# Second stage of a graph kernel: no merging between the two chunks of a step, every add behind the landing of the one ahead of it and behind two gathers

## The chip, the cores and the metric

One core of a Trainium2 chip runs the whole kernel in one launch. The metric is device time in microseconds (us), the median over runs. Engines: TensorE (PE; PEld is its weight load), VectorE (DVE), ScalarE (ACT), GpSimd (POOL), SyncE (SP, which here only issues DMAs).

## The reference

Four graph layers over the same 3125 nodes, 32 features and 100,000 edges (sorted by `dst`), each a residual `x = x + layer(relu(layernorm(x)))`:

```
_L0: agg = segment_sum(edge_attr, row, 3125); BN(relu([x, agg] @ W1.T + b1)) @ W2.T + b2
_L1: R = relu(dist * w1 + b1) @ w2 + b2                 # per edge, radial weights
     msg = R (x) Y(rel_vec) (x) features[src]           # per edge, 32 values
     out = zeros.at[dst].add(msg)
_L2: three rounds of  out = clip(0.9 * segment_sum(norm * out[row], col) + 0.1 * y, 0, 1)
_L3: three rounds of  z = BN(relu(segment_sum(wn * z[src], dst)))   # edges with a self loop per node
```

Layers L2 and L3 are done as products with dense adjacency matrices (sum of weights and number of edges for each pair src, dst), which the kernel builds itself during L0 and L1.

## The kernel before

The edges stand in 784 chunks of 128 (`CH`), of which 782 hold edges (`USED`). The program has three stages.

**First stage (L0).** Steps of four chunks; not touched by the change.

**Second stage (L1).** 196 steps (`STEPS`) of four chunks, in pairs of buffers `q = s % 2`. In step `s` of `phase1`:

- POOL fetches 128 rows of node features for each of the four chunks by an indirect DMA (`gather`, L593).
- DVE forms cross and dot products from them (L1433 is its first instruction of a step), multiplies by the radial weights (L1448, L1452), sums (L1462), and forms the values to be scattered (`products`, L1290).
- ACT builds one-hot matrices of `dst` (L668, L673); PE makes the radial weights of the step ahead (`radial`, L988) and sums the messages by node (`scatter`, L923).

**The adjacency** is a table `both` of (weight, count) pairs in DRAM, 8 bytes for each pair of nodes. Each of the 782 chunks is added to it by one indirect DMA that accumulates in place (`add(c)`, L585): 128 rows of 8 bytes. An edge that has the same key (src, dst) as another of the same chunk would be lost or doubled, so equal keys are merged first: `compare` on ACT (L656, L660) makes 128x128 matrices `same` of equal keys, DVE masks them (`mark_earlier`, L1268), PE sums the weights of equal edges (`merge`, L858, L862), and DVE writes values and rows to scatter to (`entries`, `entry_places`, L1276 to L1283). In the second stage this is done for two chunks in one go, with four matrices (chunk i against chunk j), so that the two chunks of a pair share no row, and their two adds may be under way together. The first 392 adds belong to the first stage and merge four chunks in another way.

**Order on POOL.** The stage's DMAs stand in one stream, written out without a loop: after two steps' gathers, each round issues the four gathers of step s+1 and then the two adds of the pair of step s-2 (`BEHIND`). The first add of a pair waits for both adds of the pair before to have landed, the second waits for the second add of that pair only. A step's first gather waits for `s_terms` (DVE has used the buffer two steps back).

**Third stage.** SP waits for all adds and for the last sums of the second stage, and then loads `both` back (L505), from which the dense layers L2 and L3 go on.

## Time and profile before

| | |
|---|---|
| median of 3 runs | 3463.08 us (3460.28 to 3467.24) |
| the profiled execution's own time | 3467.37 us |
| its span in the trace | 3465.3 us |
| PE, DVE, ACT, POOL busy, share of the span | 86%, 79%, 66%, 62% |
| second stage, first to last of its DVE work | about 1064 to 2820.6 us |

Busy time is given by engine. An engine that waits for a semaphore, or that stands between two instructions, is idle in it. For an indirect DMA the row of POOL is the time in which POOL makes the transfer's descriptors; the data land later.

### The profile page before, as it was taken

The numbers are of one execution on the slowest core, as the hardware profiler recorded it, in microseconds if no ns is written. First come the engines' busy times: TensorE is split into PE (matmuls) and PEld (weight loads), VectorE is DVE, ScalarE is ACT, GpSimd is POOL, SyncE is SP. The second block draws the span as 40 slices with busy tenths as digits, with TensorE's granted clock in tenths as the row PEclk, the third lists the DMA queues.
The fourth block names the chain that finished last, engine by engine and source line by source line (L and its number), as shares of the span: only waits on it lengthen the run. The fifth ranks groups of instructions, "written<-read, shape, count | busy, mean of one in ns | idle before, by whom it ended". The sixth has DMA issues, their size and how long they took to land. (4 is left out here: it accounts for less than half of the span.)

```text
span 3465.3 us, 69301 instructions
## 1 busy us (share of the span) xinstructions
PE 2974.6 (86%) x19703; PEld 2370.4 (68%) x19703; DVE 2742.9 (79%) x6018; ACT 2280.7 (66%) x3192; POOL 2141.3 (62%) x1629
## 2 busy tenths in 40 slices
PE   3888788988856999999999999999999976657657
PEld 3677677777745888888888888888888851113257
DVE  6678988888856999999999999999999973441065
ACT  3678688888836888888888888888888842220000
POOL 4048888888877777777777777777777730000000
PEclk9899899999977999999999999999999997798778
DMA  9943222222222333333333333333333359998940
GB/s 400 419 154 38 12 15 15 15 16 16 15 25 41 53 53 52 50 53 51 50 53 51 50 53 51 51 53 52 50 53 52 50 187 426 426 391 342 373 172 6
DMA packets 265695, 388.67 MB, mean 112 GB/s; under 512 B 149903, under 2 KB 200838, under 8 KB 259254
## 3 DMA queue, kind: packets, MB, share of 16 engines
q0 software_dynamic: 149184, 120.78, 20.7%
q1 hardware_dynamic: 100034, 195.42, 16.6%
q10 hardware_dynamic: 16416, 71.74, 5.1%
q8 instruction: 28, 0.46, 0.1%
q14 instruction: 33, 0.27, 0.0%
HBM read 260.01 MB, written 127.78 MB: 112 GB/s over the span
## 5 line engine op out<-in xcount | busy, mean ns | idle before, releaser
L585 POOL DMA_INDIRECT both<-kept x782 | 1333.0, 1705 | 439.8 <-issue 194.6
L923 PEld LDWEIGHTS ps<-prod,big 128*128 128x128 f32 x7840 | 1133.9, 190 | 137.7 <-DVE prod L1290 133.0
L923 PE MATMUL ps<-prod,big 128*128 128x170 f32 x7840 | 1183.2, 310 | 22.5 <-DVE prod L1290 17.4
L593 POOL DMA_INDIRECT kept<-feat_dram,kept x782 | 760.8, 973 | 243.2 <-issue 233.1
L668 ACT ACTIVATE big<-iota_b,kept 128x640 f32<-128x640 f32 x1029 | 779.0, 815 | 13.6
L914 PE MATMUL ps<-prod,onehot 128*128 128x320 f32 x3920 | 684.5, 325 | 81.2 <-DVE prod L1320 79.6
L914 PEld LDWEIGHTS ps<-prod,onehot 128*128 128x128 f32 x3920 | 597.7, 194 | 112.9 <-DVE prod L1320 84.5
L673 ACT ACTIVATE big<-big 128x2560 f32<-128x2560 f32 x196 | 458.0, 2337 | 277.2 <-PE ps L923 277.1
L988 PE MATMUL ps<-w2mix,kept 65*128 65x384 f32 x1568 | 559.3, 500 | 21.7 <-ACT kept L720 20.4
L1462 DVE TENSOR_REDUCE kept<-kept 128x80 f32<-128x1280 f32 x392 | 561.4, 1471 | 0.0
L988 PEld LDWEIGHTS ps<-w2mix,kept 65*128 65x128 f32 x1568 | 284.2, 191 | 179.7 <-issue 25.5
L1452 DVE TENSOR_TENSOR kept<-ps,kept 128x384 f32<-128x384 f32 x784 | 395.3, 544 | 0.0
L616 POOL DMA_INDIRECT prod<-both,row_idx x8 | 7.8, 977 | 526.2 <-DVE row_idx L1570 512.4
L1320 DVE TENSOR_TENSOR prod<-kept 128x1280 fp32r<-128x1280 f32 x196 | 291.9, 1489 | 4.3
L1311 DVE TENSOR_SCALAR onehot<-iota_b,kept 128x640 fp32r<-128x640 f32 x539 | 291.4, 593 | 0.0
L673 ACT ACTIVATE onehot<-big 128x640 fp32r<-128x640 f32 x196 | 171.1, 873 | 182.4 <-PE ps L914 173.7
L1129 PE MATMUL ps<-big,zring 128*32 128x512 f32 (+3 forms) x400 | 183.5, 615 | 118.6 <-DMA big<-both 106.8
L1448 DVE TENSOR_TENSOR kept<-ps,kept 128x512 f32<-128x512 f32 x392 | 266.1, 679 | 0.0
L643 ACT ACTIVATE kept<-ps,kept 128x128 f32<-128x128 f32 (+2 forms) x588 | 223.3, 477 | 0.0
L1129 PEld LDWEIGHTS ps<-big,zring 128*32 128x32 f32 x400 | 45.3, 124 | 256.8 <-issue 242.3
L1520 DVE TENSOR_REDUCE row_max<-big 128x1 f32<-128x1600 f32 x50 | 91.0, 1819 | 160.0 <-DMA adj_c<-kept 107.6
L765 ACT ACTIVATE kept<-big 128x1600 f32<-128x1600 f32 x50 | 82.2, 1648 | 187.0 <-issue 83.2
(235 smaller groups left out, 3028.9 us busy)
## 6 DMA issues: line engine op xcount, KB each, us to landing
both<-big POOLq DMA_DIRECT2D x40, 1910.0 KB, 91.2
big<-both SPq DMA_DIRECT2D x24, 1600.0 KB, 11.8
big<-both SPq DMA_DIRECT2D x24, 1528.0 KB, 13.2
kept<-keys_dram SPq DMA_DIRECT2D x196, 128.0 KB, 3.0
kept<-in_wT SPq DMA_DIRECT2D x196, 128.0 KB
adj_c<-kept ACTq DMA_DIRECT2D x42, 400.0 KB, 31.6
kept<-adj_c SPq DMA_DIRECT2D x9, 1600.0 KB, 22.4
adj_w<-kept ACTq DMA_DIRECT2D x16, 800.0 KB, 33.6
```

The costliest lines, as they stand in the source:

```text
L585: pool.indirect_dma_start(both, bass.IndirectOffsetOnAxis(ap=sc_idx[:, c:c + 1], axis=0), sc_val[:, c // 2, c % 2, :], None, compute_op=AL ...
L593: pool.indirect_dma_start(gath[:, s % 2, k, :], None, feat_dram, bass.IndirectOffsetOnAxis(ap=src_i[:, 4 * s + k:4 * s + k + 1], axis=0)). ...
L668: act.activation(dist[:, k, :], iota_b[:, :], ACT.Square, scale=-1.0, bias=bcol[:, ds(4 * s + k, 1)]).then_inc(s_dist[n], 4 // len(ks))
L673: act.activation(to[:, q, 0:len(ks), :], dist[:, 0:len(ks), :], ACT.Relu, scale=-1.0, bias=1.0).then_inc(s_oh[n], 1)
L914: mm = pe.matmul(ps[:, SUM0[part], 0:HI * 2 * FEAT], onehot0[:, q, k, part * P:(part + 1) * P], prod0[:, q, k, :, :].rearrange("p a m -> p ...
L923: mm = pe.matmul(part_sums(part, MSG), onehot[:, q, k, part * P:(part + 1) * P], prod[:, q, k, 0:HI * MSG], start=False, stop=False, skip_ ...
L988: mm = pe.matmul(ps[:, 4 + k, 0:384], hidT[:, q, k * P:(k + 1) * P], w2mix[:, :], start=True, stop=True)
L1311: ins = V.tensor_scalar(onehot0[:, q, k, :], iota_b[:, :], b_src[:, ds(4 * s + k, 1)], None, ALU.is_equal)
L1320: V.tensor_tensor(prod0[:, q, :, :, :], high0[:, ds(4 * s, 4), :].unsqueeze(3) .broadcast_to([P, 4, HI, 2 * FEAT]), rows0[:, 4 * k4:4 * k4 ...
L1448: V.tensor_tensor(T[:, :, 0:256].rearrange("p k (o x) -> p k o x", o=16), ps[:, 4 + 2 * g:6 + 2 * g, 0:256].rearrange("p k (o x) -> p k o ...
L1452: ins = V.tensor_tensor(T[:, k, 256:640].rearrange("p (u i x) -> p u i x", u=8, i=3), ps[:, 4 + 2 * g + k, 256:384].rearrange("p (u x) -> ...
L1462: V.tensor_reduce(res[:, q, 2 * g:2 * g + 2, 0:40], terms[:, g, :, :].rearrange("p k (o x) -> p k o x", x=16), AX, ALU.add).then_inc(s_red, 1)
```

## The change

`compare` makes two matrices instead of four (each chunk only against itself: two squares of 128 columns instead of two of 256, one relu of 256 instead of 512), and `merge` has two matmuls fewer (four instead of six). `mark_earlier` reads two adjacent matrices instead of the first and the fourth. Since two chunks of a pair may now hold the same row, each add of the second stage waits for the landing of the one just ahead of it (`s_add` of the other parity), and on POOL one add now stands behind each two gathers instead of two adds behind four. The number of gathers and adds is the same.

```diff
             def add(c):
 
                 pool.wait_ge(s_idx, c // 2 + 1)
-                if c >= CH // 2 and c % 2 == 0:
-                    pool.wait_ge(s_add[1], 16 * (c // 2))
-                if c >= 2:
+                if c >= CH // 2:
+                    pool.wait_ge(s_add[(c - 1) % 2], 16 * ((c + 1) // 2))
+                if 2 <= c <= CH // 2:
                     pool.wait_ge(s_add[c % 2], 16 * (c // 2))
...
             for s in range(STEPS + BEHIND):
-                if s + 1 < STEPS:
-                    gather(s + 1, range(min(4, USED - 4 * (s + 1))))
-                if s >= BEHIND:
-                    for c in range(2 * (STEPS + s - BEHIND), min(2 * (STEPS + s - BEHIND) + 2, USED)):
+                for k in range(4):
+                    if s + 1 < STEPS and 4 * (s + 1) + k < USED:
+                        gather(s + 1, k)
+                    c = 2 * (STEPS + s - BEHIND) + k // 2
+                    if s >= BEHIND and k % 2 and c < USED:
                         add(c)
...
                 for i in range(2):
-                    act.activation(key_gap[:, 2 * i * P:(2 * i + 2) * P], keyrow[:, q, 0:2 * P], ACT.Square, scale=-1.0,
+                    act.activation(key_gap[:, i * P:(i + 1) * P], keyrow[:, q, i * P:(i + 1) * P], ACT.Square, scale=-1.0,
                                    bias=key[:, ds(2 * d + i, 1)]).then_inc(s_gap, 1)
...
-                act.activation(same[:, q, 0:4, :].rearrange("p b e -> p (b e)"), key_gap[:, 0:4 * P], ACT.Relu,
+                act.activation(same[:, q, 0:2, :].rearrange("p b e -> p (b e)"), key_gap[:, 0:2 * P], ACT.Relu,
                                scale=-1.0, bias=1.0).then_inc(s_same, 1)
...
                 for j in range(2):
-                    pe.matmul(o[:, j, 0:1], same_tri[:, q, j, :], ones_bf[:, :], start=(j == 0), stop=False,
+                    pe.matmul(o[:, j, 0:1], same_tri[:, q, j, :], ones_bf[:, :], start=(j == 0), stop=True,
                               skip_group_check=True)
-                    for i in range(2):
-                        lo = 0 if (i, j) == (0, 1) else 1
-                        mm = pe.matmul(o[:, j, lo:7], same[:, q, 2 * i + j, :],
-                                       wparts[:, ds(2 * d + i, 1), lo:7].rearrange("p c v -> p (c v)"),
-                                       start=False, stop=(i == 1), skip_group_check=True)
+                    mm = pe.matmul(o[:, j, 1:7], same[:, q, j, :],
+                                   wparts[:, ds(2 * d + j, 1), 1:7].rearrange("p c v -> p (c v)"),
+                                   start=False, stop=True, skip_group_check=True)
```

POOL's stream at the second stage's first rounds with adds, before: L593 is a gather, L585 an add, and the semaphores `entries_added0` and `entries_added1` count the landings of adds with even and odd numbers.

```order
418 L593 DMA kept<-feat_dram,kept 128x96 [waits terms_ready]
419 L593 DMA kept<-feat_dram,kept 128x96 x3
420 L585 DMA both<-kept 9779712x2 [waits entries_added0,entries_added1,scatter_rows_ready]
421 L585 DMA both<-kept 9779712x2 [waits entries_added1,scatter_rows_ready]
422 L593 DMA kept<-feat_dram,kept 128x96 [waits terms_ready]
423 L593 DMA kept<-feat_dram,kept 128x96 x3
```

The same place of the change, where a gather is L592 (the file is one line shorter from there on). One add now follows each two gathers, and it waits for the add of the other parity.

```order
418 L592 DMA kept<-feat_dram,kept 128x96 [waits terms_ready]
419 L592 DMA kept<-feat_dram,kept 128x96
420 L585 DMA both<-kept 9779712x2 [waits entries_added0,entries_added1,scatter_rows_ready]
421 L592 DMA kept<-feat_dram,kept 128x96 x2
422 L585 DMA both<-kept 9779712x2 [waits entries_added0,scatter_rows_ready]
423 L592 DMA kept<-feat_dram,kept 128x96 [waits terms_ready]
424 L592 DMA kept<-feat_dram,kept 128x96
425 L585 DMA both<-kept 9779712x2 [waits entries_added1,scatter_rows_ready]
```

The end of POOL's second stage, before: behind the last two gathers stand the last six adds, in pairs.

```order
1186 L593 DMA kept<-feat_dram,kept 128x96 [waits terms_ready]
1187 L593 DMA kept<-feat_dram,kept 128x96
1188 L585 DMA both<-kept 9779712x2 [waits entries_added0,entries_added1,scatter_rows_ready]
1189 L585 DMA both<-kept 9779712x2 [waits entries_added1,scatter_rows_ready]
1190 L585 DMA both<-kept 9779712x2 [waits entries_added0,entries_added1,scatter_rows_ready]
1191 L585 DMA both<-kept 9779712x2 [waits entries_added1,scatter_rows_ready]
1192 L585 DMA both<-kept 9779712x2 [waits entries_added0,entries_added1,scatter_rows_ready]
1193 L585 DMA both<-kept 9779712x2 [waits entries_added1,scatter_rows_ready]
```

The end of the change: the same six adds, each of which waits for the one just ahead.

```order
1378 L592 DMA kept<-feat_dram,kept 128x96 [waits terms_ready]
1379 L592 DMA kept<-feat_dram,kept 128x96
1380 L585 DMA both<-kept 9779712x2 [waits entries_added1,scatter_rows_ready]
1381 L585 DMA both<-kept 9779712x2 [waits entries_added0,scatter_rows_ready]
1382 L585 DMA both<-kept 9779712x2 [waits entries_added1,scatter_rows_ready]
1383 L585 DMA both<-kept 9779712x2 [waits entries_added0,scatter_rows_ready]
1384 L585 DMA both<-kept 9779712x2 [waits entries_added1,scatter_rows_ready]
1385 L585 DMA both<-kept 9779712x2 [waits entries_added0,scatter_rows_ready]
```

## Rows read from the trace of the kernel before

**Rows 1.** The page, part 1: busy us, share of the span, instructions.
```profile
PE 2974.6 (86%) x19703; PEld 2370.4 (68%) x19703; DVE 2742.9 (79%) x6018; ACT 2280.7 (66%) x3192; POOL 2141.3 (62%) x1629
```

**Rows 2.** Busy us by stretch, with granted clock, DMA share and GB/s.
```profile
1600.00:2800.00 1200.00, 1184.85 (x7235) 990.52 (x7234) 1137.14 (x2680) 996.80 (x1341) 955.06 (x804) 1.00 0.32 51
```

**Rows 3.** Waits from 1600 to 2800 us: total us, times, longest us.
```profile
POOL kept L593 <- issue: 161.2, 529, 0.3
...
DVE kept L1433 <- DMA kept<-feat_dram,kept: 25.5, 93, 0.4
```

**Rows 4.** Groups by line, 1600 to 2800 us: busy us, mean ns, idle before.
```profile
L593 POOL DMA_INDIRECT kept<-feat_dram,kept x536 | 519.7, 970 | 163.3 <-issue 161.2 <-DMA both<-kept 2.1
L585 POOL DMA_INDIRECT both<-kept x268 | 435.8, 1626 | 81.7 <-issue 43.6 <-DVE kept L1283 38.1
```

**Rows 5.** POOL in order of time, one step: start us, us, instruction, [idle before].
```profile
2021.00 1.01 POOL L593 DMA_INDIRECT kept<-feat_dram,kept  x1 [0.30 <-issue]
2022.31 0.98 POOL L593 DMA_INDIRECT kept<-feat_dram,kept  x1 [0.30 <-issue]
2023.60 0.94 POOL L593 DMA_INDIRECT kept<-feat_dram,kept  x1 [0.30 <-issue]
2024.84 0.94 POOL L593 DMA_INDIRECT kept<-feat_dram,kept  x1 [0.30 <-issue]
2026.09 1.61 POOL L585 DMA_INDIRECT both<-kept  x1 [0.30 <-DVE kept L1283]
2028.00 1.58 POOL L585 DMA_INDIRECT both<-kept  x1 [0.30 <-issue]
```

**Rows 6.** All engines in order of time, DVE's start of the next step.
```profile
2027.52 0.26 DVE L1433 TENSOR_TENSOR kept<-kept 128x96 f32<-128x96 f32 x1 [0.33 <-DMA kept<-feat_dram,kept]
```

**Rows 7.** POOL where a long run of adds changes to gathers.
```profile
1055.73 1.54 POOL L585 DMA_INDIRECT both<-kept  x1 [0.30 <-issue]
1057.58 1.02 POOL L593 DMA_INDIRECT kept<-feat_dram,kept  x1 [0.30 <-issue]
...
1060.19 0.94 POOL L593 DMA_INDIRECT kept<-feat_dram,kept  x1 [0.30 <-issue]
```

**Rows 8.** POOL, the last gather of the stage that DVE held up.
```profile
1095.52 1.01 POOL L593 DMA_INDIRECT kept<-feat_dram,kept  x1 [0.49 <-DVE kept L1452]
```

**Rows 9.** POOL in the stage before, an add that waits for the second add ahead.
```profile
1041.08 1.54 POOL L585 DMA_INDIRECT both<-kept  x1 [0.34 <-issue]
...
1045.78 1.54 POOL L585 DMA_INDIRECT both<-kept  x1 [1.11 <-DMA both<-kept]
```

**Rows 10.** All engines at the second stage's end, in order of time.
```profile
2802.68 1.61 POOL L585 DMA_INDIRECT both<-kept  x1 [0.30 <-issue]
...
2803.30 0.17 PE L858 MATMUL ps<-ones_bf,kept 128*128 128x1 bf16 x1
...
2803.45 2.83 PE L988 MATMUL ps<-w2mix,kept 65*128 65x384 f32 x8
...
2804.59 1.63 POOL L585 DMA_INDIRECT both<-kept  x1 [0.30 <-issue]
...
2808.48 1.56 POOL L585 DMA_INDIRECT both<-kept  x1 [2.26 <-DMA both<-kept]
...
2810.34 1.54 POOL L585 DMA_INDIRECT both<-kept  x1 [0.30 <-issue]
...
2814.07 1.80 POOL L585 DMA_INDIRECT both<-kept  x1 [2.19 <-DMA both<-kept]
...
2816.17 1.54 POOL L585 DMA_INDIRECT both<-kept  x1 [0.30 <-issue]
2820.64 0.32 DVE L1484 TENSOR_TENSOR x<-x,ps 128x160 f32<-128x160 f32 x1 [6.19 <-PE ps L923]
2820.82 35.73 SPq L505 DMA_DIRECT2D big<-both  x10
```

**Rows 11.** The line of the adds, 1600 to 2800 us: durations in ns, min/median/max.
```profile
L585 POOL DMA_INDIRECT both<-kept x268: 1582/1610/1689, 1604.7 to 2798.2; - x134
```

More of the change, by code:

```diff
@@ L586, in add, with gather @@
                                         sc_val[:, c // 2, c % 2, :], None, compute_op=ALU.add).then_inc(s_add[c % 2], 16)
-            def gather(s, ks):
-                if s >= 2:
+            def gather(s, k):
+                if s >= 2 and k == 0:
                     pool.wait_ge(s_terms, 2 * (s - 1))
-                for k in ks:
-                    pool.indirect_dma_start(gath[:, s % 2, k, :], None, feat_dram,
-                                            bass.IndirectOffsetOnAxis(ap=src_i[:, 4 * s + k:4 * s + k + 1], axis=0)
-                                            ).then_inc(s_gath[s % 2], 16)
+                pool.indirect_dma_start(gath[:, s % 2, k, :], None, feat_dram,
+                                        bass.IndirectOffsetOnAxis(ap=src_i[:, 4 * s + k:4 * s + k + 1], axis=0)
+                                        ).then_inc(s_gath[s % 2], 16)
             pool.wait_ge(s_zeroed, 16 * (ZERO_PIECES + 1))
@@ L601, in _ @@
             pool.wait_ge(s_feat, 16)
-            gather(0, range(4))
+            for k in range(4):
+                gather(0, k)
             for s in range(STEPS + BEHIND):
-                if s + 1 < STEPS:
-                    gather(s + 1, range(min(4, USED - 4 * (s + 1))))
-                if s >= BEHIND:
-                    for c in range(2 * (STEPS + s - BEHIND), min(2 * (STEPS + s - BEHIND) + 2, USED)):
+                for k in range(4):
+                    if s + 1 < STEPS and 4 * (s + 1) + k < USED:
+                        gather(s + 1, k)
+                    c = 2 * (STEPS + s - BEHIND) + k // 2
+                    if s >= BEHIND and k % 2 and c < USED:
                         add(c)
@@ L1267, in mark_earlier @@
                 dve.wait_ge(s_ded, d - 1)
-                V.tensor_tensor(same_tri[:, q, 0:2, :], same[:, q, 0:4:3, :], earlier[:, :].unsqueeze(1).broadcast_to([P, 2, P]),
+                V.tensor_tensor(same_tri[:, q, 0:2, :], same[:, q, 0:2, :], earlier[:, :].unsqueeze(1).broadcast_to([P, 2, P]),
                                 ALU.mult).then_inc(s_tri, 1)
```

## The prediction

> **What bounds the kernel now.** Read the page first, part 1: PE is the busiest engine by far and POOL the least busy [rows 1]. That is an average over three stages, and the change touches the second alone. The chain that ended last is no help here, since on this page it can be followed only from 3128 us on, behind the stage. So take a stretch in the middle of the stage, 1600 to 2800 us. Of its 1200 us PE is busy 1184.85, DVE 1137.14, ACT 996.80 and POOL 955.06, at a granted clock of 1.00, the higher level of 2.4 GHz [rows 2]. By busy time PE would be the bound, and POOL would have 20% to spare.
>
> The waits say otherwise. Ahead of the gathers POOL's idle time comes in pieces of at most 0.3 us [rows 3], and ahead of the adds it is 81.7 / 268 = 0.30 on average [rows 4]. The groups give the sum too: gathers 519.7 busy and 163.3 idle before them, adds 435.8 and 81.7, together 1200.5 us of the 1200 [rows 4]. So POOL never waits for anybody; 0.30 us is what lies between two of its indirect DMAs in any case. The stretch holds 268 / 2 = 134 steps, so a step takes 1200.5 / 134 = 8.96 us, and that is POOL's own sum: four gathers, two adds, six gaps. DVE, on the contrary, waits at the head of its step for the gathered rows, in 93 of the 134 steps [rows 3]: the last gather starts at 2024.84 and DVE, after 0.33 us of waiting for it, at 2027.52 [rows 5, 6]. PE and ACT wait for DVE and for each other behind it. **POOL is the bound of the stage**, from the last gather that DVE held up, at 1095.52 [rows 8], to the stage's end. It covers 190 steps.
>
> Now look at one step of POOL closely [rows 5]. The four gathers do the same work, but take 1.01, 0.98, 0.94 and 0.94 us. The first after an add is 0.07 us longer, the second 0.04, and from the third on there is nothing more. The same stands where a run of nearly 400 adds ends: 1.02 for the first gather, 0.94 for the third [rows 7]. The adds have it too: 1.61 for the first after a gather, 1.58 for the second, 1.54 in a long run [rows 5, 7]. A change of kind costs POOL about 0.11 us over two instructions.
>
> **The change part by part.**
>
> *ACT.* Two squares and a relu with half the columns. ACT is busy 996.80 of 1200 us, so it has room already: 0 us. What hides it is POOL's step; nothing is late next.
>
> *PE.* Two bf16 matmuls fewer for each step. Six of them stand between 2803.30 and 2803.45, where the next matmul begins [rows 10], so two are worth 0.05 us a step. PE works in POOL's shadow: 0 us. Were PE the bound it would be 0.05 x 190 = 9.5 us less.
>
> *DVE.* As many instructions of the same size: 0 us.
>
> *The new wait for landing.* Behind it stand on POOL two gathers and the next add, and DVE's next step waits for these gathers. The trace before shows what a landing takes where POOL has nothing else to do: an add that starts at 2804.59 lets the next but one start at 2808.48, 3.89 us later; another at 2810.34 lets it start at 2814.07, 3.73 us later [rows 10]. In the changed stream the next add can't start earlier anyway than 1.61 + 0.30 + 1.01 + 0.30 + 0.98 + 0.30 = 4.50 us after the one ahead. So the wait is over 0.6 us before it could hold anything: 0 us a step. The bounds are 3.73 and, from the stage before, 4.70 us (1041.08 to 1045.78 [rows 9]), where two adds of a quick row of adds were under way together. At 4.70 each add would stall 0.20 us. I take 3.8, because the changed adds stand apart by two gathers and never share the queue with another add.
>
> By the Trainium skill ("DMA: Bandwidth & Descriptors", the section on the anatomy of a DMA on the GpSimd path), a small transfer of this kind has about 2.0 us of fixed cost, most of it the receipt of the write; as an estimate by that page the wait would end 2 us ahead of need, and the sum would be the same. The rows say 3.7 to 3.9, and only 0.6 us of cover is left.
>
> *The order on POOL.* Here is the cost. Six instructions a step as before, but four changes of kind instead of two. The third and fourth gather, 0.94 and 0.94, come to stand as first and second after an add, 1.01 and 0.98: + 0.07 + 0.04 = 0.11 us a step. Both adds now stand as first after a gather; the row of before has 1.61 and 1.58, which would be 0.03 more, but the group's mean of 1.626 [rows 4] lies above both, so the second is no cheaper on average: 0. Together 0.11 x 190 = 20.9 us. The bounds: 0 below, if the durations do not follow the position, and 0.14 x 190 = 26.6 above, with the adds' 0.03.
>
> *The end of the stage.* Six adds stand behind the last gather. Before, they ran in pairs, and from the first of them (2802.68) to SP's first load of the third stage (2820.82) it was 18.14 us; DVE saw PE's last sum at 2820.64, so both sides ended together [rows 10]. Now they go one by one: five times 3.73 to 3.89, and then from the last start to SP's load as before 4.65 us (2816.17 to 2820.82), or some 3.1 if that landing was a late one. That is 18.65 + 3.1 = 21.8 to 19.45 + 4.65 = 24.1 us, against 18.14: + 3.6 to 6.0, taken as 4.5. On the other side, an add now stands between the last gather of the last full step and the last two gathers, so this gather is 1.9 us nearer to the end, and DVE's and PE's last two steps with it: + 1.9, hidden beside the adds' 4.5. SP's loads wait for both, and the third stage waits for the loads.
>
> *Sum.* 20.9 + 4.5 = 25.4 us. Against the profiled execution's own 3467.37 us that is 3492.8. Its time is 4.3 above the median of the runs, so the forecast is 3463.1 + 25.4 = 3488.5, given as **3488 us**, 0.7% slower.
>
> **The rivals.**
>
> *A. One add does not undo what two gathers have set up.* In the trace an add between gathers always comes in twos or more, so what a single one does is not shown. If the cost of 0.07 is made of 0.03 for the instruction just ahead and 0.04 for the one before that, the first gather after a single add pays 0.03 and the second 0.04: 0.14 a step instead of 0.11. With the adds' 0.03 or without it that is 0.03 to 0.06 x 190 = 6 to 11 us, and with the end 10 to 16: 3473 to 3479 us. That the second instruction still pays speaks for it; that two gathers are already enough to make the next add dear (1.61 at 2802.68) speaks for neither.
>
> *B. The position costs nothing new.* The durations follow something else that the new order does not change, and only the end of the stage is left: 3463.1 + 4.5 = 3467.6, and 3465 if a part of it is hidden in the third stage. This is within 0.2%, which is 6.9 us and about what a measurement of this kernel can tell from no change. Against it speaks that two different places show the same 0.07 and 0.04.
>
> *C. The landing is not covered.* It decides from 4.50 us on. At the 4.70 of rows 9, each add stalls 0.20: 0.40 x 190 = 76 us more, 3564. A stall in one of four adds gives 19 us more, 3507. For it: the loads of SP lie in the same part of a step. Against it: 3.73 and 3.89, and an add in the new order has the same neighbours ahead (two gathers) as the first add of a pair before.
>
> *D. POOL is not the bound; its rows only fill the step.* Then PE is, at 1184.85 of 1200 us, and the two matmuls are a gain: 3463.1 - 9.5 = 3453.6, 0.3% faster, if PE's last step also hides the adds' end. Against it: POOL's gaps are 0.30 to the last digit and its gathers agree to 0.01 us in each position, which a stretched engine would not show, and DVE waits for the gathers. It would decide only if PE's own step were above 8.96 us.
>
> *E. The adds' durations move with what DVE does beside them.* They spread from 1.58 to 1.69 us [rows 11]. If the moved add fell wholly on 1.54 [rows 7] or on 1.68 instead of its mean of 1.626, it would be -0.09 or +0.05 a step, -16 or +10 us: 3472 to 3498. The Trainium skill ("SBUF — State Buffer", the section on its two separate sides) has a rule of that form: DVE and GpSimd take one port pair in turn for a whole instruction, DVE's with two operands in SBUF included. By this rule, the trace agrees as far as that the adds spread; the gathers, which stand beside DVE as well, do not.
>
> **How the numbers follow.** Forecast 3488, own range 3480 to 3496: 0.47. A: 0.20. B: 0.13. C: 0.07. D: 0.05. E: 0.08. The range 3466 to 3498 holds the forecast, A, E and the upper half of B; what it leaves out is C, D and the rest of B, some 0.18. Faster by over 0.2% are D and a sliver of B and E together: 0.06. Within 0.2% is B and the lower edge of A: 0.16. Slower: 0.78.
>
> **What the profile of the changed kernel would show.** POOL's rows in the middle of the stage: gather, gather, add, with 1.01, 0.98, 1.61 and gaps of 0.30; busy plus idle still the whole stretch; a step of 9.07 us. A shows as a first gather of 0.97, B as 0.94. C shows as gaps above 0.30 before adds, ended by the DMA both<-kept. D shows as POOL waiting for DVE, with a step below 8.96. DVE's idle time before its first instruction of a step should grow by what POOL's step does. The last six adds should start 3.7 to 3.9 us apart, and SP's load 22 to 24 us behind the first of them. The third stage should keep its length of 645 us. The prediction is wrong if the step is not 0.1 us longer, or if the gap before the adds is.

## The result, and the profile after

The changed kernel takes **3516.44 us** (median of 4 runs, 3510.75 to 3520.16), the kernel before on the same chip 3465.16 us. The ratio is 1.0149 (95% interval 1.0127 to 1.017): 51 us or 1.5% slower, twice the 25.4 us forecast, and above the range. The profiled execution took 3514.57 us, with a span of 3512.5, 47.2 more than that of before.

The page, part 1, answers to [rows 1], and busy time by stretch for 1600 to 2800 us to [rows 2]:

```profile
PE 2977.3 (85%) x19310; PEld 2377.0 (68%) x19311; DVE 2740.9 (78%) x6018; ACT 2198.1 (63%) x3192; POOL 2151.1 (61%) x1629
```

```profile
1600.00:2800.00 1200.00, 1156.39 (x6783) 972.30 (x6783) 1108.18 (x2612) 916.82 (x1307) 940.63 (x784) 0.99 0.31 50
```

Every engine does less in the same 1200 us. The stage has become slower without a busier engine, so something is waited for: ahead of an instruction, or inside one. The groups of POOL for the same stretch, against [rows 4] (busy us, mean ns of one, idle before them and what ended it):

```profile
L592 POOL DMA_INDIRECT kept<-feat_dram,kept x522 | 508.7, 974 | 159.2 <-issue 110.7 <-DMA both<-kept 48.5
L585 POOL DMA_INDIRECT both<-kept x262 | 433.5, 1655 | 100.5 <-issue 60.1 <-DVE kept L1282 22.3 <-DMA both<-kept 18.2
```

The stretch holds 262 / 2 = 131 steps; POOL's four sums make 1201.9 us, or 9.175 a step against 8.959. By terms: gathers 508.7 / 131 = 3.883 (before 3.878), adds 3.309 (3.252), idle time 259.7 / 131 = 1.982 (1.828). So + 0.005, + 0.057 and + 0.154, together 0.216 a step, and times 190 that is 41 us. (Busy and idle time fill any stretch, so the sum alone doesn't show that POOL is the bound. `z2_nudged_more`, below, does: there an add that takes 0.6 us longer makes the step 9.48 us.) The waits and the durations of the adds' line say how it is spread:

```profile
POOL both L585 <- issue: 60.1, 169, 1.5
...
DVE kept L1432 <- DMA kept<-feat_dram,kept: 53.9, 100, 2.1
...
POOL both L585 <- DMA both<-kept: 18.2, 20, 1.2
```

```profile
L585 POOL DMA_INDIRECT both<-kept x262: 1597/1607/2301, 1598.6 to 2798.0; - x131
```

Before, no idle time on POOL was above 0.3 us; now the longest ahead of an add is 1.5. And while the median add still takes 1607 ns, the longest takes 2301 instead of 1689 [rows 11]. Below, an add is called *stalled* when POOL stands idle for more than 0.35 us ahead of it (0.30 lie between two of its DMAs in any case), and *held* when it takes over 1.7 us. Two steps in order of time show both; these are the rows of POOL, SP and DVE's `products` from all engines' (start, duration, [idle before]):

```profile
1999.32 1.61 POOL L585 DMA_INDIRECT both<-kept  x1 [0.31 <-DVE kept L1282]
1999.40 0.87 DVE L1289 TENSOR_TENSOR prod<-high,kept 128x680 f32<-128x680 f32 x1 [0.23 <-DVE kept L1470]
...
2000.63 0.34 SPq L424 DMA_DIRECT2D kept<-keys_dram  x1
...
2001.23 0.98 POOL L592 DMA_INDIRECT kept<-feat_dram,kept  x1 [0.30 <-issue]
2001.86 0.49 SPq L468 DMA_DIRECT2D kept<-in_wT  x1
2002.51 0.95 POOL L592 DMA_INDIRECT kept<-feat_dram,kept  x1 [0.30 <-issue]
2004.44 1.60 POOL L585 DMA_INDIRECT both<-kept  x1 [0.98 <-DMA both<-kept]
2006.35 0.98 POOL L592 DMA_INDIRECT kept<-feat_dram,kept  x1 [0.31 <-issue]
2007.63 0.95 POOL L592 DMA_INDIRECT kept<-feat_dram,kept  x1 [0.30 <-DMA both<-kept]
...
2008.61 0.87 DVE L1289 TENSOR_TENSOR prod<-high,kept 128x680 f32<-128x680 f32 x1 [0.23 <-DVE kept L1470]
...
2008.89 2.07 POOL L585 DMA_INDIRECT both<-kept  x1 [0.30 <-issue]
...
2018.10 0.87 DVE L1289 TENSOR_TENSOR prod<-high,kept 128x680 f32<-128x680 f32 x1 [0.23 <-DVE kept L1470]
2018.25 2.19 POOL L585 DMA_INDIRECT both<-kept  x1 [0.30 <-issue]
```

*A landing that comes late.* The add at 1999.32 lets the next one start at 2004.44, 5.12 us later, with 0.98 instead of 0.30 us ahead of it. SP issued two loads of 128 KB, keys (L424) and weights (L468), 1.31 and 2.54 us after the add's start.

*An add that is held.* The add at 1999.32 starts 0.08 us before `products` and takes 1.61. Those at 2008.89 and 2018.25 start 0.28 and 0.15 us after it and take 2.07 and 2.19. Both end at the same distance from the start of `products`: 0.28 + 2.07 = 2.35 and 0.15 + 2.19 = 2.34 us.

Where nothing disturbs, the add is the first of the two by more (the same view, later):

```profile
2056.18 1.65 POOL L585 DMA_INDIRECT both<-kept  x1 [0.30 <-DVE kept L1282]
2056.57 0.87 DVE L1289 TENSOR_TENSOR prod<-high,kept 128x680 f32<-128x680 f32 x1 [0.23 <-DVE kept L1470]
```

The end of the stage answers to [rows 10]:

```profile
2841.10 1.60 POOL L585 DMA_INDIRECT both<-kept  x1 [0.30 <-issue]
2844.84 1.57 POOL L585 DMA_INDIRECT both<-kept  x1 [2.15 <-DVE kept L1282]
2850.03 1.54 POOL L585 DMA_INDIRECT both<-kept  x1 [3.61 <-DMA both<-kept]
2854.76 1.54 POOL L585 DMA_INDIRECT both<-kept  x1 [3.19 <-issue]
2858.47 1.54 POOL L585 DMA_INDIRECT both<-kept  x1 [2.17 <-DMA both<-kept]
...
2862.28 1.54 POOL L585 DMA_INDIRECT both<-kept  x1 [2.27 <-DMA both<-kept]
2867.16 20.07 SPq L505 DMA_DIRECT2D big<-both  x7
```

From the first of the six adds to SP's load it is 26.06 us, against 18.14: + 7.9 instead of the 4.5 forecast. Three of the five distances are 3.7 to 3.8 us, the other two 5.19 and 4.73. The third stage keeps its length, 3512.5 - 2867.2 = 645.3 us. With the 41 us above that makes 49 us, against 47.2 measured. In three other kernels with the same end it was less: 24.1 us in `x0_after_again`, 24.3 in `x2_late_loads` and 24.4 in `x5_late_split`, which is + 6.0 to 6.2.

### The profile page after: what moved, and what is told of

It reads as the page before. It is cut to its first block and busy times, and to the rows that moved or that the text cites. A ratio compares the mean times of both kernels' runs of the same rounds, so it can differ in the third digit from the quotient of the medians.

```text
span 3512.5 us, 68324 instructions
## 1 busy us (share of the span) xinstructions
PE 2977.3 (85%) x19310; PEld 2377.0 (68%) x19311; DVE 2740.9 (78%) x6018; ACT 2198.1 (63%) x3192; POOL 2151.1 (61%) x1629
## 5 line engine op out<-in xcount | busy, mean ns | idle before, releaser
L585 POOL DMA_INDIRECT both<-kept x782 | 1341.4, 1715 | 475.7 <-issue 224.8
L922 PEld LDWEIGHTS ps<-prod,big 128*128 128x128 f32 x7840 | 1152.6, 193 | 173.9 <-DVE prod L1289 166.8
L922 PE MATMUL ps<-prod,big 128*128 128x170 f32 x7840 | 1198.6, 313 | 64.8 <-DVE prod L1289 61.2
L592 POOL DMA_INDIRECT kept<-feat_dram,kept x782 | 762.3, 975 | 243.6 <-issue 164.9
```

The source lines that it names most:

```text
L585: pool.indirect_dma_start(both, bass.IndirectOffsetOnAxis(ap=sc_idx[:, c:c + 1], axis=0), sc_val[:, c // 2, c % 2, :], None, compute_op=AL ...
L592: pool.indirect_dma_start(gath[:, s % 2, k, :], None, feat_dram, bass.IndirectOffsetOnAxis(ap=src_i[:, 4 * s + k:4 * s + k + 1], axis=0)). ...
L922: mm = pe.matmul(part_sums(part, MSG), onehot[:, q, k, part * P:(part + 1) * P], prod[:, q, k, 0:HI * MSG], start=False, stop=False, skip_ ...
```

## The experiments

Ratios are against the kernel before on the same chip, with 95% intervals. In the expectations an odd add is the one behind a round's last gather, an even add the one in its middle.

**First: which part of the change costs?** Four kernels. `e1_order` has the merging and the waits of before and only the new order:

```diff
...
-                if s + 1 < STEPS:
-                    gather(s + 1, range(min(4, USED - 4 * (s + 1))))
-                if s >= BEHIND:
-                    for c in range(2 * (STEPS + s - BEHIND), min(2 * (STEPS + s - BEHIND) + 2, USED)):
+                for k in range(4):
+                    if s + 1 < STEPS and 4 * (s + 1) + k < USED:
+                        gather(s + 1, k)
+                    c = 2 * (STEPS + s - BEHIND) + k // 2
+                    if s >= BEHIND and k % 2 and c < USED:
                         add(c)
```

> Merging, matmuls and waits as in the kernel before; only POOL's order is the changed one (one add behind each two gathers). My first prediction (a change of kind costs 0.07 + 0.04 us) expects a step of 9.07 us and 3486 us. The theory that the wait for landing is the cost, and the order alone is free (changed kernel: gathers 0.98 and 0.95, adds 1.60 and 1.61), expects 0.98 x 2 + 0.95 x 2 + 1.60 + 1.61 + 6 x 0.305 = 8.90 us a step, no gap above 0.31 before an add, the end of the stage as before, and 3453 to 3462 us.

Measured: 3481.49 us, 1.0061 (1.004 to 1.0081). `e2_order_wait` has the new order and the new waits, with the merging of before (shown: the waits):

```diff
...
-                if c >= CH // 2 and c % 2 == 0:
-                    pool.wait_ge(s_add[1], 16 * (c // 2))
-                if c >= 2:
+                if c >= CH // 2:
+                    pool.wait_ge(s_add[(c - 1) % 2], 16 * ((c + 1) // 2))
+                if 2 <= c <= CH // 2:
                     pool.wait_ge(s_add[c % 2], 16 * (c // 2))
...
```

> The kernel before with the changed order and with the wait of each add for the one ahead, but with the merging of both chunks kept (four matrices, six matmuls). If order and wait are the whole cost, the time is that of the changed kernel, 3516, within 5 us. If the shorter compare on ACT matters, because it lets SP issue its 128 KB load of keys 0.2 us earlier and so into the landing of the add, this kernel has fewer stalls: gap before even adds 0.31 to 0.36 instead of 0.47, and 3475 to 3490 us.

Measured: 3496.32 us, 1.0097 (1.0073 to 1.0122). `e3_wide_compare` is the changed kernel with ACT's comparison as wide as before (the relu is widened too, and the readers of `same` take the first and the fourth matrix):

```diff
-                    act.activation(key_gap[:, i * P:(i + 1) * P], keyrow[:, q, i * P:(i + 1) * P], ACT.Square, scale=-1.0,
+                    act.activation(key_gap[:, 2 * i * P:(2 * i + 2) * P], keyrow[:, q, 0:2 * P], ACT.Square, scale=-1.0,
...
```

> The changed kernel, with ACT's compare as wide as before (four matrices made, two of them unused) and the matmuls of the change. It tells ACT's part from PE's. If the earlier load of keys is the cause, the time is that of the run with merging kept (3475 to 3490). If ACT has no part, it is 3516 within 5 us.

Measured: 3492.0 us, 1.0104 (1.0061 to 1.0147). `e4_pairs_wait` is the changed kernel with the order of before, where nothing covers the second add's wait:

```diff
...
-                for k in range(4):
-                    if s + 1 < STEPS and 4 * (s + 1) + k < USED:
-                        gather(s + 1, k)
-                    c = 2 * (STEPS + s - BEHIND) + k // 2
-                    if s >= BEHIND and k % 2 and c < USED:
+                if s + 1 < STEPS:
+                    gather(s + 1, range(min(4, USED - 4 * (s + 1))))
+                if s >= BEHIND:
+                    for c in range(2 * (STEPS + s - BEHIND), min(2 * (STEPS + s - BEHIND) + 2, USED)):
                         add(c)
```

> The changed kernel with the old order: four gathers, then two adds, each add waiting for the one ahead. The second add has no gather in front of it, so the landing stands open: 3.7 to 3.9 us from one start to the next instead of 1.92, which is 1.8 to 2.0 us a step and 340 to 380 us in all, 3810 to 3860 us. If a landing were covered by something else, it would stay near 3516.

Measured: 3894.32 us, 1.1254 (1.122 to 1.1289), above the 3810 to 3860 expected. Its POOL in order of time, one pair of adds:

```profile
2003.82 1.63 POOL L585 DMA_INDIRECT both<-kept  x1 [0.30 <-issue]
...
2007.73 1.59 POOL L585 DMA_INDIRECT both<-kept  x1 [2.29 <-DMA both<-kept]
```

3.91 us from add to add, in the middle of the stage; half of the pairs lie between 3.83 and 4.23 us, and the longest is 5.5. What follows from the four: the new order alone already costs. With the waits too it is a little more (the two intervals overlap), and the changed kernel, with the *shorter* work of ACT and PE, is slower still (its interval overlaps that of `e3_wide_compare`, and not those of `e1_order` and `e2_order_wait`; its second measurement, `x0_after_again` below, overlaps none of the three). No sum of fixed prices per instruction gives this: in `e1_order` a gather takes 974 ns on average as in the changed kernel, where I forecast dearer ones. In the profiled execution, the slowest of the seven, it is the adds that are longer, 3.374 us a step against 3.252, more than twice what the idle time has grown by (1.880 against 1.828):

```profile
L585 POOL DMA_INDIRECT both<-kept x263 | 443.7, 1687 | 87.1 <-issue 63.9 <-DVE kept L1284 23.2
```

`e1_order` isn't the order alone, though. In it the even add still waits for the odd one ahead, and there are now two gathers between them instead of four: that old wait has lost half of its cover, which is the time that passes between an add and the one that waits for it anyway.

**Second: loads and products.** My theory from here on: (1) SP's loads delay an add's landing beyond its cover; (2) an add that starts within `products` is held. Four edits of the changed kernel, and the kernel itself again. `x1_shifted` moves each add one gather ahead, away from `products`; `x2_late_loads` lets SP load a step's keys only when DVE has taken the step ahead; `x3_shifted_late` does both; `x4_split_products` forms the products by two instructions of half the size (edits in this order):

```diff
-                    if s >= BEHIND and k % 2 and c < USED:
+                    if s >= BEHIND and k % 2 == 0 and c < USED:
```

```diff
+                if not first(s):
+                    sp.wait_ge(s_vec, s - 1)
                 load_keys(s + STEPS, q)
```

```diff
-                V.tensor_tensor(prod[:, q, :, 0:HI * MSG].rearrange("p k (a m) -> p k a m", a=HI),
+                for k in (0, 2):
+                    V.tensor_tensor(prod[:, q, k:k + 2, 0:HI * MSG].rearrange("p k (a m) -> p k a m", a=HI),
...
```

> The changed kernel itself again, beside the others on one chip: 1.0127 to 1.017 times the kernel before, as measured. Its odd adds (those behind the last gather of a step) start within 0.9 us of DVE's products in part of the steps and take up to 2.3 us there.

> The changed kernel with each add one gather earlier on POOL (gather, add, gather, gather, add, gather): the same number of gathers between two adds, the same waits, but no add near the start of DVE's products (4.5 us before or 0.3 us after their end). Theory of the lock (an add that starts in the first 0.7 us of the products is held until 0.75 us after their start): no add above 1.75 us, 20 to 35 us less than the changed kernel. Theory that the cost is a change of kind on POOL or the landing alone: adds as long as before, same time within 8 us.

> The changed kernel, with SP's two 128 KB loads of a step held back until DVE has formed its vectors (about 1.5 us later). Theory that these loads delay the landing of the add behind the last gather: landings of odd adds as early as of even ones (3.1 us from the start), gap before even adds 0.31 instead of 0.47, 20 to 30 us less than the changed kernel. If the landing is late for another reason (gathers behind it), no change within 8 us.

> Both edits in the changed kernel: one gather earlier, and SP's loads held back. If lock and landing are the two causes, the step comes to 8.90 to 8.95 us and the time to that of the kernel before plus the end of the stage (some 8 us): 1.000 to 1.003 of it.

> The changed kernel with DVE's products of a step made by two instructions of half the size. In the trace of the changed kernel an add that starts up to 0.7 us behind the start of the products ends at 2.35 us behind it, whatever its start. If the add is held for as long as one DVE instruction runs, no add is longer than 1.61 + 0.3 = 1.9 us (2.3 in the changed kernel), the mean of odd adds falls from 1.71 to 1.65 and the time by 5 to 15 us, less what the second instruction costs where DVE is late. If the add's length has another cause (DMA rings, the loads), the longest stay at 2.3.

| kernel | us (runs) | ratio |
|---|---|---|
| `x0_after_again` | 3511.77 (4) | 1.0193 (1.0158 to 1.0227) |
| `x1_shifted` | 3511.37 (4) | 1.0178 (1.0158 to 1.0198) |
| `x2_late_loads` | 3478.43 (6) | 1.0083 (1.0066 to 1.01) |
| `x3_shifted_late` | 3642.59 (4) | 1.0557 (1.0539 to 1.0574) |
| `x4_split_products` | 3502.76 (4) | 1.0122 (1.0095 to 1.0148) |

The late loads give back 33 us of 58. In the profiled execution, the fastest of six, POOL's adds are undisturbed (its line, and its group, 1600 to 2700 and 1600 to 2800 us):

```profile
L587 POOL DMA_INDIRECT both<-kept x246: 1597/1607/1660, 1602.5 to 2699.6; - x123
```

```profile
L587 POOL DMA_INDIRECT both<-kept x268 | 430.9, 1608 | 84.8 <-issue 43.4 <-DVE kept L1284 39.3 <-DMA both<-kept 2.1
```

`x3_shifted_late` went the opposite way of its expectation, and says most. I had thought of the loads as harmful near the end of the add's descriptors and of the new place as clear of that. Its waits and rows:

```profile
POOL both L587 <- DMA both<-kept: 129.7, 112, 1.9
```

```profile
2002.19 1.69 POOL L587 DMA_INDIRECT both<-kept  x1 [0.30 <-issue]
2003.30 0.34 SPq L424 DMA_DIRECT2D kept<-keys_dram  x1
2003.84 0.48 SPq L470 DMA_DIRECT2D kept<-in_wT  x1
...
2007.71 1.60 POOL L587 DMA_INDIRECT both<-kept  x1 [1.29 <-DMA both<-kept]
```

The keys load comes 1.11 us after the add's start, and it takes 5.52 us to the next add. In the changed kernel (above) it was 1.31 us and 5.12, and in `x0_after_again`, POOL and SP in order of time, 1.43 us and 4.67:

```profile
2012.67 1.61 POOL L585 DMA_INDIRECT both<-kept  x1 [0.30 <-DVE kept L1282]
...
2014.10 0.34 SPq L424 DMA_DIRECT2D kept<-keys_dram  x1
...
2017.34 1.60 POOL L585 DMA_INDIRECT both<-kept  x1 [0.46 <-issue]
```

The traces also hold the times at which an add's semaphore is counted up; the last of them is its landing. For the adds of the twelve traces in which two gathers stand between two adds (`e1` to `e3`, `x0` to `x5`, `y1`, `y4` and the changed kernel), held ones left out (1600 to 2790 us):

| keys load issued, us after the add's start | adds | landing, us after the add's start: median (10% to 90%) |
|---|---|---|
| no load from 1.5 us before to 3 us after | 1555 | 3.03 (2.95 to 3.11) |
| 0.1 to 0.5 | 102 | 3.53 (3.37 to 3.88) |
| 0.5 to 0.9 | 157 | 3.81 (3.63 to 4.14) |
| 0.9 to 1.3 | 139 | 4.49 (4.19 to 4.77) |
| 1.3 to 1.5 | 76 | 3.87 (3.52 to 4.41) |
| 1.5 to 1.7 | 130 | 3.33 (3.00 to 3.63) |
| 1.7 to 1.9 | 228 | 3.15 (3.03 to 3.38) |
| 1.9 to 3.0 | 420 | 3.05 (2.96 to 3.14) |

Of 358 stalls in these traces, 298 end 0.77 us after the landing of the add ahead, which is late beside the loads or because that add was held. So a landing later than about 3.7 us stalls the next add. The same two loads, moved by about a microsecond, cost 131 us in one order (`x3_shifted_late` against `x1_shifted`) and give 33 in the other: (1) is shown. `y1_merged_shifted` (below) has the load at 0.6 us and no stall, but there the next add doesn't wait for that one.

The table also shows how ACT's shorter comparison can cost. SP's keys load waits for ACT's squares, so it comes earlier, as the expectations of `e2_order_wait` and `e3_wide_compare` had it. In steps without disturbance it comes 1.77 to 1.79 us (median) after the add with the wide comparison (`e1_order`, `e2_order_wait`, `e3_wide_compare`) and 1.50 to 1.57 with the narrow one (`x0_after_again`, the changed kernel), where landings get near the limit: stalls were 14 to 19 there and 42 to 43 here.

The other 60 stalls the theory did not have. In each of these traces but `y1` the wait ends 1.78 us (2.08 in `x1` and `x3`) after the landing at one add in 54 (one in 36 in `x1` and `x3`), always the same ones of an order; call these periodic. The changed kernel has seven of them in the stage, about a microsecond each, so up to 7 of the 51 us. What they are is not known.

`x1_shifted` missed by 20 to 35 us. The held adds went but for six (mean 1621 instead of 1655 ns), but now gathers are held, up to 1622 instead of 1136 ns; their mean is 991 instead of 974. One of them starts 0.08 us after `products`:

```profile
L592 POOL DMA_INDIRECT kept<-feat_dram,kept x524 | 519.4, 991 | 159.7 <-issue 111.5 <-DMA both<-kept 47.8 <-DVE kept L1451 0.4
```

```profile
1900.35 0.87 DVE L1289 TENSOR_TENSOR prod<-high,kept 128x680 f32<-128x680 f32 x1 [0.23 <-DVE kept L1470]
1900.43 1.61 POOL L592 DMA_INDIRECT kept<-feat_dram,kept  x1 [0.30 <-DMA both<-kept]
```

And stalls took the place of the rest, since the shifted even add now stands beside the loads; the longest, up to 2.0 us, are periodic. `x4_split_products` bears out (2): each of the two instructions takes 0.51 us instead of 0.87, held adds end 1.99 to 2.00 us after the start of the first instead of 2.35, which is 1.48 us after its end in both kernels, and the longest add falls from 2.30 to 1.94 us.

```profile
L585 POOL DMA_INDIRECT both<-kept x262: 1597/1608/1943, 1601.4 to 2799.9; - x131
```

**Third: the order by itself, and what is left.** `y3_before_late` is the kernel before with the late loads, `y4_order_late` is `e1_order` with them, `y1_merged_shifted` has the merging and waits of before with the adds behind the first and third gather, `x5_late_split` is the changed kernel with late loads and split products (edits as above).

> The kernel before, with SP's loads held back as in the late-loads run. Its POOL never waits and has four gathers of cover, so the later loads should change nothing: 0.999 to 1.001 of the kernel before, a step of 8.95 us. If it becomes faster, SP's loads cost something on a path that is not the landing of the adds.

> Merging, matmuls and waits of the kernel before, the changed order of POOL, and SP's loads held back. Sum from the changed kernel's undisturbed rows: 2 x 0.98 + 2 x 0.95 + 1.60 + 1.61 + 6 x 0.305 = 8.90 us a step against 8.95, the stage's end as before: 8 to 10 us faster than the kernel before, 0.997 of it. If the order itself costs something beside landing and lock, it is not faster.

> Merging, matmuls and waits of the kernel before, and POOL's order gather, add, gather, gather, add, gather. The add that lands late (the one behind the first gather, beside SP's loads) is waited for only by the add two further on, and no add starts in the first 0.7 us of DVE's products. If landing and lock are all that the changed order costs, there is no gap above 0.31 and no add above 1.75 us, the step is 8.90 us against 8.95, and the time 0.997 of the kernel before, 8 to 10 us less. If the order has a cost of its own, the time is above that of the kernel before.

> The changed kernel with both remedies: SP's loads held back (landings), and the products in two instructions (lock). Expected if these two are the whole cost inside the step: a step of 8.92 to 8.96 us, and what is left is the end of the stage, some 8 us: 1.002 to 1.004 of the kernel before. If something else is at work it stays at 1.008 or above.

| kernel | us (runs) | ratio |
|---|---|---|
| `y3_before_late` | 3456.16 (10) | 0.9995 (0.9981 to 1.001) |
| `y4_order_late` | 3482.71 (8) | 1.0077 (1.0052 to 1.0102) |
| `y1_merged_shifted` | 3458.85 (12) | 0.9992 (0.9975 to 1.0009) |
| `x5_late_split` | 3474.3 (10) | 1.0031 (1.0017 to 1.0044) |

`x5_late_split` leaves 10.7 us by its ratio, of which the end of the stage is 6.2 in its own trace. With both causes treated, the middle of the stage costs some 4.5 us. `y1_merged_shifted` has four changes of kind a step, and from 1600 us on no holds, and no stall before the stage's end. Its groups on POOL:

```profile
L592 POOL DMA_INDIRECT kept<-feat_dram,kept x533 | 516.1, 968 | 162.6 <-issue 162.6
L585 POOL DMA_INDIRECT both<-kept x272 | 436.8, 1606 | 87.1 <-issue 81.4 <-DMA both<-kept 5.7
```

By the means, four gathers and two adds with their gaps are 4 x 0.968 + 2 x 1.606 + 4 x 0.305 + 2 x 0.320 = 8.94 us, against 8.96. **Changes of kind cost nothing.** Nor is `y1_merged_shifted` a measured gain; 8 to 10 us less had been expected. What costs is where an order puts its adds.

`y4_order_late` missed (0.997 was expected). Its loads are out of the way and its landings are on time, and yet it is as slow as `e1_order`. From 1717 to 1821 and from 2207 to 2463 us its odd adds were held in most steps; the line for the second of these stretches from 2217 us on, and POOL in order of time where the first one begins:

```profile
L587 POOL DMA_INDIRECT both<-kept x53: 1598/1791/2202, 2217.0 to 2462.7; - x53
```

```profile
1712.56 1.60 POOL L587 DMA_INDIRECT both<-kept  x1 [0.72 <-issue]
...
1717.02 2.14 POOL L587 DMA_INDIRECT both<-kept  x1 [0.30 <-issue]
```

The stall of the even add at 1712.56 is a periodic one, and the next odd add is the first that is held. The second series begins in the same way, behind the periodic stall at 2203.04; behind the one at 1960.71 nothing is held. In `e1_order` a held add follows each of the five periodic stalls between 1600 and 2790 us, and series of 13 and 19 follow two of them.

**Fourth: do holds feed themselves?** The rows of the changed kernel suggest it. `products` at 2018.10 comes 10.47 us after the start of the round's last gather at 2007.63, and that at 2008.61 10.54 us after the one at 1998.07. That gather (at 1998.07 in the same view) stands *ahead* of the held add. So `products` comes on time, the next add comes late by what the hold cost, lands within `products` once more, and is held again. To test it without loads, landings or the new order, the kernel before gets one nudge of POOL in step 60: one memset of 224 columns (`z1_nudged`, in step 130 as well), two of 224 (`z2_nudged_more`, shown), four of 112 (`z3_nudged_four`, which also names eight semaphores that nothing uses).

```diff
+                if s == 60:
+                    for n in range(2):
+                        pool.memset(nudge[:, n, :], 0.0)
                 if s + 1 < STEPS:
```

> The kernel before, and ahead of the gathers of rounds 60 and 130 one memset of 224 columns on POOL, which puts POOL back by about 0.5 us each time. Theory that the lock feeds itself (an add held makes the step longer, the next products start earlier beside the next add, and this add is held as well): behind each nudge the first add of a step takes 1.8 to 2.3 us and the step 9.4 us for ten steps or many more, 5 to 60 us in all. If each hold is an accident of its own, the two nudges cost 1 us together and the step behind them is 8.95 at once.

> The kernel before with two memsets of 224 columns on POOL ahead of the gathers of round 60. One memset had put POOL back by only 0.17 us, less than the 0.24 us that the add starts ahead of the products. If two put it back by 0.25 to 0.9 us, the theory of a state that feeds itself expects the first adds of the steps behind it to take 1.8 to 2.3 us, for ten steps or more; single accidents expect one such add at most.

> The same with four memsets of 112 columns, for a longer delay (some 0.5 to 1.0 us). If the next add then starts within the first 0.7 us of the products, the self-feeding state expects a run of long adds behind it; if the delay is longer than that, the add starts behind the products and nothing is held.

`z1_nudged`: 3463.27 us, 0.9999 (0.9982 to 1.0016). Its memset of 0.87 us lay mostly beside an add and put POOL back by only 0.17 us: inconclusive. `z2_nudged_more`, POOL in order of time:

```profile
1590.05 1.65 POOL L586 DMA_INDIRECT both<-kept  x1 [0.30 <-issue]
1591.12 1.11 POOL L607 MEMSET nudge<- 128x224 f32 x2
1592.39 1.02 POOL L594 DMA_INDIRECT kept<-feat_dram,kept  x1 [0.16 <-issue]
...
1597.51 2.20 POOL L586 DMA_INDIRECT both<-kept  x1 [0.30 <-issue]
...
1606.99 2.15 POOL L586 DMA_INDIRECT both<-kept  x1 [0.30 <-issue]
```

One delay (the gather starts at 1592.39 instead of some 1592.0), and the first add of the pair is long in 14 steps in a row. The line before and after 1725 us:

```profile
L586 POOL DMA_INDIRECT both<-kept x28: 1582/1844/2209, 1597.5 to 1722.6; - x28
```

```profile
L586 POOL DMA_INDIRECT both<-kept x218: 1582/1610/1706, 1729.6 to 2698.9; - x109
```

So a single disturbance of 0.4 us was paid for again and again, in the untouched order. In the times it is lost in the scatter: 1.0017 (0.9985 to 1.0048). One execution took 3490.79 us, the kernel before's there not above 3467.68, but no trace says why. `z3_nudged_four` (3464.7 us, 1.0023, 1.0 to 1.0045) put POOL back by nearly the same, 0.47 us, and had three held adds in a row and then none. Each is one trace. So a hold can feed itself; for how long was not found.

## Why the prediction was wrong

**Right:** POOL is the bound of the stage (its delays lengthen the step, and DVE's wait for its gathers grows by the step's 0.22 us, so rival D is out); the savings on ACT and PE bring nothing by themselves; the six last adds one by one; a third stage of 645 us; the sign.

**Wrong, the step that failed: the new wait for landing, put at "0 us a step".** The price of 3.73 to 3.89 us was read at the end of the stage [rows 10], where SP issues no more loads. In the middle it depends on when SP's keys load is issued: in the examples at 1.1 to 1.4 us after the add's start it is 4.7 to 5.5, and the cover is 1.60 + 0.30 + 0.98 + 0.30 + 0.95 + 0.30 = 4.4 us. So 44 of the 262 adds stalled, and POOL's idle time grew by 0.154 us a step instead of 0. This is the mechanism of rival C, to which I gave 0.07 although it named SP's loads; its own case, every add at 4.70, didn't come, and its other one, a stall in one of four adds (3507), was the nearest of all. The wait that was there already, even add behind odd, had its cover cut from four gathers to two by the new order, and I didn't look at it. `e1_order`, without any new wait, has gaps of up to 1.1 us ahead of adds. They are the smaller part of its 0.6%, holds the larger, and how much the old wait costs by itself was not measured. The prediction's estimate from the 2.0 us of the Trainium skill ("DMA: Bandwidth & Descriptors", the section on the anatomy of a DMA on the GpSimd path) was a little off too: 4.50 less 2.0 is 2.5 us, not 2. Nothing hung on it.

**Wrong: "Here is the cost", 20.9 us for the changes of kind.** A gather behind a single add takes 0.98 and the next 0.95 us, not 1.01 and 0.98, and an add takes 1.60 or 1.61. A pair of gathers is 1.93, less than rival A's 1.95, and `y1_merged_shifted` is no slower than before. The gathers' real term in the profile after is + 0.005 us a step.

**Wrong in size: rival E.** The adds' durations do move with DVE, but not by the - 0.09 to + 0.05 that it allowed [rows 7, 11]. In the rows of before, the first add of each pair starts 0.22 to 0.41 us ahead of `products`. That margin was nowhere in my working. Past it the price is up to 0.7 us an add, and it can come again in the next step. The prediction has gathers exempt; they are not, only that in the kernel before none of them starts within `products`. The Trainium skill ("SBUF — State Buffer", "SBUF: two separate sides") says that of a DVE instruction with two operands in SBUF and a GpSimd one that reads SBUF, whichever starts first has the shared ports for the whole instruction. By this rule the trace agrees: adds that start 0.08 us or more ahead of `products` are free, held ones end 1.48 us after the end of the DVE instruction whether it takes 0.87 or 0.51 us, and held gathers too end at a fixed distance, 1.7 us after its start. At which point a DMA's instruction needs the ports is not shown: a whole add takes 1.60 us, and not 1.48.

**Mis-sized: the end, + 7.9 instead of + 4.5.** Two of five landings took 5.19 and 4.73 us and not 3.8. The second is at the same add as in `x0_after_again`, `x2_late_loads` and `x5_late_split` (4.59, 4.74, 4.70), where the end is + 6.0 to 6.2; the first was not seen there, and what delayed it was not tried.

**How the causes share the 51 us.** The stage's end has 7.9. The rest, some 41 to 43, is idle time of POOL (0.154 of 0.216 a step in the profile) and longer adds (0.057), but they are not two prices. A stall of a few tenths pushes the next add behind the start of `products`, the holds follow; and where a hold shifts POOL against SP, the next landing meets the loads elsewhere. Each cure alone gives part: late loads 33 us; split products between 9 and 24 going by the two measurements of the changed kernel, and by the first of them the two intervals overlap. Both together leave 10.7, of which the middle of the stage has 4.5.

**Open:** by what path SP's loads delay a landing; what makes the same add wait a microsecond longer in every 54; what ends a series of holds, and why some stalls start a long one and others none.

## What to carry to other kernels

A landing has no price of its own: read it where the other queues do what they do at the place of the new wait, and look at the old waits too when an order changes, since each lives on the instructions between it and its release. In a loop whose engines keep fixed distances, note the smallest margin between two instructions that share ports, because a disturbance larger than it can be paid again in the steps that follow (14 here). Moving the instruction that is held may only put another in its place. When a stage gets slower and no engine gets busier, look at the maximum and not the mean of each line.

## What the runs showed of the hardware

- An indirect DMA that adds 128 rows of 8 bytes takes POOL 1.60 us, and up to 2.30 when it starts up to about 0.7 us after the start of a DVE instruction of 0.87 us with two operands in SBUF; it then ends 2.35 us after that start (1.99 to 2.00 where the DVE instruction takes 0.51). A gather of 128 rows, 0.95 to 0.98 us, took up to 1.62 in the same place.
- Such an add landed 3.03 us after its start on quiet queues, and an add that waited for it started 0.77 us later. When another queue issued the first of two loads of 128 KB 0.9 to 1.3 us after the start it landed at 4.49 us, at 0.5 to 0.9 us 3.81, and from 1.9 us on there was no delay (medians).
- At one add in 54, always the same, the wait ended 1.78 us after the landing instead of 0.77.
- A delay of 0.4 us on POOL, once, lengthened 14 steps in a row in one trace, and a delay of 0.47 us three.
